# Next-row maxima on a transformer kernel: one 128-row product each, or pairs of 48-row products

## The reference

```python
xn = layernorm(x)
# branch 1: causal attention with a bump instead of a softmax, 16 heads of 8
pressure = q @ k.T * scale ; pressure = where(causal, -10000, pressure)
energy = (pressure - phase_threshold) / (softplus(compressibility) + 1e-6)
attn = 1 - tanh(energy) ** 2 ; attn /= attn.sum(-1) + 1e-6
s = (attn @ v) @ Wo.T
# branch 2: softmax attention (16 heads of 8), then a mixture of experts
h = rmsnorm(xn, norm1_w)
X = xn + softmax(q2 @ k2.T * scale) @ v2 @ wo
h2 = rmsnorm(X, norm2_w)
# shared expert, plus the top 2 of 8 experts weighted by a softmax of their probabilities
ffn = X + swiglu_shared(h2) + sum_e combine[:, e] * swiglu_e(h2)
out = x + s * silu(ffn)
```

## Time and profile before

| | us |
|---|---|
| median of 3 runs | 1097.45 (1096.49 to 1097.86) |
| the profiled execution, its own time | 1097.14 |
| its span, first to last instruction | 1095.4 |
| TensorE busy | 990.9 (90%) |
| VectorE busy | 831.4 (76%) |
| ScalarE busy | 646.8 (59%) |
| GpSimd busy | 351.2 (32%) |

### The profile page before, as it was taken

The page is one execution under the profiler, slowest core; times in us unless marked ns, Lnnn a source line. Parts: engine busy times, 40 slices in busy tenths (PEclk is TensorE's granted clock), DMA queues, the critical chain, the costliest instruction groups (busy, mean ns, idle before and its releaser), DMA issues.

```text
span 1095.4 us, 18252 instructions
## 1 busy us (share of the span) xinstructions
PE 990.9 (90%) x6763; PEld 467.3 (43%) x6784; DVE 831.4 (76%) x1684; ACT 646.8 (59%) x882; POOL 351.2 (32%) x211
## 2 busy tenths in 40 slices
PE   4489999899998999889998999989999899988997
PEld 1123464245542455324652346523554245532464
DVE  6885977869776888759878598795977779773962
ACT  3569724786258842698336972379624785258731
POOL 4702443033520355105530154203352033610032
PEclk9589999999999999999999999999999999999999
DMA  7350561023700435105331055211471033600020
GB/s 231 71 109 22 111 169 34 21 55 80 190 20 12 99 93 132 30 2 130 112 83 30 2 130 143 51 31 30 101 181 24 21 79 83 163 20 2 1 79 10
DMA packets 60392, 81.83 MB, mean 75 GB/s; under 512 B 8560, under 2 KB 47728, under 8 KB 57296
## 3 DMA queue, kind: packets, MB, share of 16 engines
q1 hardware_dynamic: 56544, 75.61, 28.3%
q10 hardware_dynamic: 3760, 5.05, 1.4%
HBM read 52.98 MB, written 27.39 MB: 73 GB/s over the span
## 4 chain that ended last, share of the span: by engine, by line
PE 53%; DVE 25%; ACT 12%; issue 4%; DMA 2%; SPq 1%; ACTq 0%; POOL 0%; DVEq 0%; POOLq 0%
PE O L1156 11%; DVE nmax L758 10%; DVE PT L813 9%; PE O L1139 7%; ACT PT L613 7%; PE S L1172 6%; PE S L1174 5%; PE S L1173 5%; PE S L1112 4%; PE M L1075 3%; PE M L1054 2%; PE M L1080 1%; PE O L1075 1%; SPq L368 1%; DMA stackQ<-mTZ 1%
## 5 line engine op out<-in xcount | busy, mean ns | idle before, releaser
L613 ACT ACTIVATE PT<-S 128x1024 f32<-128x1024 f32 (+1 forms) x448 | 417.0, 967 | 113.7 <-PE S L1112 108.7
L813 DVE SCALAR_TENSOR_TENSOR PT<-PT 128x768 f32<-128x768 f32 (+1 forms) x192 | 213.4, 1163 | 101.0 <-ACT PT L613 101.0
L758 DVE TENSOR_REDUCE nmax<-M 128x1 f32<-128x512 f32 x329 | 218.2, 684 | 43.2 <-PE M L1075 28.3
L1139 PE MATMUL O<-PT,V 128*32 128x256 f32 (+3 forms) x2816 | 246.5, 430 | 0.0
L494 POOL TENSOR_TENSOR PT<-PT,CB 128x1024 f32<-128x1024 f32 x56 | 133.6, 2392 | 261.2 <-DVE PT L951 146.9
L646 ACT ACTIVATE PT<-S 128x1024 f32<-128x1024 f32 x72 | 73.9, 1027 | 241.4 <-PE S L1174 241.4
L479 POOL TENSOR_TENSOR split<-split,parts 128x512 f32<-128x512 f32 x30 | 90.9, 3029 | 372.0 <-ACT parts L573 372.0
L1112 PE MATMUL S<-stackQ,stackK 64*128 64x512 bf16 (+3 forms) x1024 | 166.3, 347 | 9.5 <-DMA stackQ<-mTZ 5.3
L758 DVE TENSOR_REDUCE nmax<-O 128x1 f32<-128x512 f32 x183 | 125.1, 684 | 36.5 <-PE O L1075 17.6
L1172 PE MATMUL S<-h2hi,wgu_hi 128*128 128x512 f32 x288 | 148.7, 516 | 4.3 <-DVE PT L951 4.2
L1156 PE MATMUL O<-PT,wdn 128*128 128x512 f32 x288 | 142.9, 595 | 0.9
(11 more groups left out here) (198 smaller groups left out, 1044.5 us busy)
## 6 DMA issues: line engine op xcount, KB each, us to landing
CB<-scrC SPq DMA_DIRECT2D x64, 256.0 KB, 5.6
stackQ<-scrQ SPq DMA_DIRECT2D x30, 384.0 KB, 5.5
stackK<-scrK SPq DMA_DIRECT2D x30, 384.0 KB, 6.3
scrQ<-parts SPq DMA_DIRECT2D x32, 192.0 KB, 3.3
scrK<-parts SPq DMA_DIRECT2D x30, 192.0 KB, 5.9
scrQ<-parts SPq DMA_DIRECT2D x32, 128.0 KB, 3.4
scrK<-parts SPq DMA_DIRECT2D x30, 128.0 KB, 5.2
KX<-scrK SPq DMA_DIRECT2D x14, 192.0 KB, 3.4
```

What stands on the lines that cost most here:

```text
L613: a.activation(PT[:, n % SLOTS, 2 * q * w:2 * q * w + 2 * w].rearrange("p (r n) -> p r n", r=2), S[k][:, :].rearrange("p (r n) -> p r n", ...
L758: v.tensor_reduce(nmax[:, h % 2, h // 2, t:t + 1], M[k][:, :], AX.X, ALU.max, negate=True).then_inc(m_read[k], 1)
L813: v.scalar_tensor_tensor(p, p, 1.0, p, ALU.subtract, ALU.mult).then_inc(weighed, 1)
L1139: last = t_.matmul(O[k][32 * q:32 * q + VW, i0:i1], V[:, j, 4 * g + q, :], PT[:, n % SLOTS, w * q + at:w * q + at + i1 - i0], start=(j == ...
```

## The change

The maxima X and W of the next row take the paired form as well, so that `maximum` has one form only. `KX`, its clearing on GpSimd, its semaphore and its two DMAs a row are dropped, and the first maximum of run X waits for `stack["K2"]` in its place. So that no pair is torn over two experts or by another piece of work, run X is spread as 4, 4, 4, 4 over experts 2 to 5 (5, 4, 4, 3 before), and `ctxT1` moves behind the fourth maximum of expert 4.

```diff
-PADDED = 4
-spread(MAX["X"], {EXPERT + e: n for e, n in enumerate((0, 0, 5, 4, 4, 3))})
+spread(MAX["X"], {EXPERT + e: n for e, n in enumerate((0, 0, 4, 4, 4, 4))})
 spread(MAX["W"], {EXPERT + 5 + e: n for e, n in enumerate((2, 6, 6, 2))})
 PLACES[EXPERT + 4].insert(2, "V1")
-PLACES[EXPERT + 4].insert(4, "ctxT1")
+PLACES[EXPERT + 4].insert(5, "ctxT1")
...
-        KX = sb("KX", [128, 2, PADDED, L], bf16)
...
             engine.wait_ge(stored[name], (bt + 1) * STORED)
-            if name == "K2" and (not isinstance(bt, int) or bt > 0):
-                for r in range(2):
-                    engine.dma_start(KX[HALF * r:HALF * r + ROW_ADD, r, :, :],
-                                     scratch[name][r].rearrange("c (d h) n -> (c d) h n", h=HP)[:, 0:PADDED, :]).then_inc(stacked_KX, 16)
             load_heads(engine, name, 0, HP, stacked[name])
...
-            g.memset(KX[:, :, :, :].bitcast(dt.uint32), 0).then_inc(kset, 1)
...
             def maximum(u, it, name):
 
                 _m, h, t = name
-                a, hp = HALF * (h % 2), h // 2
+                hp = h // 2
                 rows_later = name in MAX["X"] or name in MAX["W"]
-                alone = rows_later and u is not FIRST
-                if not alone and h % 2:
+                if h % 2:
                     return
-                banks = [begin(u, ("max", i, t)) for i in ((h,) if alone else (h, h + 1))]
+                banks = [begin(u, ("max", i, t)) for i in (h, h + 1)]
                 if 2 in banks:
                     pe.wait_ge(o_read[1], (it + rows_later) * O_USES[1] + 1)
-                if alone:
-                    t_.matmul(M[banks[0]][:, :], stack["Q2"][:, hp, t * 128:t * 128 + 128], KX[:, h % 2, hp, :],
-                              start=True, stop=True).then_inc(m_full[banks[0]], 1)
-                    return
                 for r, k in enumerate(banks):
                     rows = slice(HALF * r, HALF * r + ROW_ADD)
                     t_.matmul(M[k][:, :], stack["Q2"][rows, hp, t * 128:t * 128 + 128], stack["K2"][rows, hp, :],
                               start=True, stop=True).then_inc(m_full[k], 1)
...
-                            pe.wait_ge(stacked_KX, bt * 32)
+                            pe.wait_ge(stacked["K2"], (bt + 1) * 32)
```

More of the change, by code:

```diff
@@ L272, in program @@
         stacked = {n: sem("stacked" + n) for n in stack}
-        stacked_KX = sem("stacked_KX")
         opened = sem("opened")
@@ L400, in prepare @@
                     sp.wait_ge(setup, 2)
-                    sp.wait_ge(kset, 4)
+                    sp.wait_ge(kset, 3)
                     for name in ("Q1", "K1"):
@@ L517, in row @@
                     weigh_expert(it, e)
-            pool.wait_ge(kset, 4)
+            pool.wait_ge(kset, 3)
             pool.wait_ge(gu_hi, 2)
```

## The result

The changed kernel takes 1110.61 us (median of 4 runs, 1109.14 to 1110.72) against 1097.65 (4 runs, 1096.49 to 1099.26): ratio 1.0114, 95% interval 1.0096 to 1.0131. It is slower by 13.0 us, clear of noise, and inside the stated range of 1101.5 to 1113.5. The forecast was 1107.5, with 0.60 on 1104.5 to 1110.5; the measured median lies 0.1 us above that inner band.

What follows compares the result with a forecast made beforehand. TensorE was taken to bound experts 2 to 8. Pairs +0.80 and waits +0.68 gave +1.5 us a row, times seven +10.4, on 1097.14: 1107.5 us; range 1101.5 to 1113.5, with 0.60 on 1104.5 to 1110.5.

Steps and rivals of the forecast that it cites:

- The bound: Experts 2 to 8: TensorE is busy 43.38 of 44 us, so a shift of the experts' end carries one to one.
- The price of a single and of a pair: In the experts: single 0.23 us, pair 0.51 against 0.46 for two singles; 16 pairs give +0.80 us a row.
- The drain: Around each pair: switching array shape drains the engine; 0.29 us of the pair's 0.51 is the two switches.
- The waits: Experts 2 to 8: pairs needing two of three banks at once raise TensorE's waits from 0.7 to 1.36, +0.68 a row.
- Up f0 of expert 2: TensorE's wait before this product falls to 0.24 us from 0.50, since the pair ahead lies in the old wait.
- maxT_X: TensorE's wait before this product rises to 0.34 us from 0.2, its bank being read only after VectorE's 1.39 us cast.
- The wait in expert 3: Heads 0 and 1, tile 3: the pair waits 0.27 us for a VectorE read that stands behind the `oT1` work.
- my walk: Experts 2 to 8, stepped through with TensorE's step times and VectorE's queue; with pairs it ends at +1.49 us a row.
- What costs nothing: Waiting for `stack["K2"]` (12 us of cover), dropping `KX`'s DMAs and clearing, and moving `ctxT1` by 0.9 us: nothing.
- The switches are not hidden: Denies the rival of hidden switches in the experts: pair 0.23, -4.6 us in all, 1092.5; turning point 0.31; faster: 0.06.
- only the price of the pair counts: Rival, in the experts: all added waits vanish, +0.8 us a row, 1102.7; chance 0.14 for 1101.5 to 1104.5.
- the waits bite harder: Rival, experts 4 to 7: VectorE's order reacts, +2.1 us a row, 1111.8, at twice that 1116; chance 0.14 above 1110.5.

Runs made afterwards that it cites:

- e1: The kernel before, with VectorE's maxima of the next row (runs X and W) reading only 64 of 512 columns: 1096.86 us, ratio 1.0004.
- e2: The changed kernel with the same short reads, 64 of 512 columns in runs X and W of the next row: 1103.92 us, ratio 1.0055 to before.
- e4: The kernel before in its own order, each single of runs X and W of the next row as a lone 48-row product: 1155.06 us, ratio 1.0528.
- e3: The changed kernel's order, banks and waits, each pair as two 128-row products against the zero-padded copy of K: 1105.28 us, ratio 1.0072 to before.
- e5: The changed kernel with the padded copy of K still cleared and loaded but read by nobody: 1108.35 us, ratio 1.0087 to before.
- e6: The changed kernel with only the clearing of the padded copy on GpSimd kept, no transfers: 1112.02 us, ratio 1.0119 to before.
- e9: The changed kernel run once more, unchanged, for a second profile of its start: 1109.46 us (one run).
- e10: The kernel before run once more, unchanged, on the same chip: 1099.17 us (one run).

## Why the prediction was right, and where it was off

**The bound.** Right. TensorE fills experts 2 to 8, and the stretch from the ruler's end to the next row's first gate product is 74.4 us before and 74.5 after (means of seven): what the experts gain in length goes one to one into the row.

**The price of a single and of a pair.** Right, the sign of the result hangs on it. 0.23 and 0.51 were read from edges elsewhere in the trace, and one pair in place reads 0.52. The sum over a row was low: taking the change of waits (0.35) off 1.53 leaves 1.18 for the pairs, where the working had 0.80; the same from e1 and e2, +0.87 with waits of 0.53 in e1 and 0.25 in e2, gives 1.15. Some of it is that a pair is 0.52 rather than 0.51 (0.2 a row), some that a single behind L1156 costs 0.22 (before, a single at 412.46 and the second product behind it, L1173, at 412.91, less one step of 0.23), not 0.23. That split is worked out and not tested by itself, and a part stays open; what the rulers give is the sum: a pair is 0.07 dearer than two singles, where the working had 0.05.

**The drain.** The rule of the Trainium skill ("TensorEngine Tiling (Array Packing)", Key Properties), that a change of tiling mode drains the engine, agrees with e4: 0.26 to 0.27 us for a switch there and back around a lone product. How much of that is emptying the engine and how much a weight load that is no longer hidden, no run separates. The "Up to 2×" of the Trainium skill ("TensorEngine Tiling (Array Packing)", Theoretical Speedup) is borne out within the pair, whose halves start within 0.01 us; with the switches around it the pair is slower than two singles here.

**The waits.** The mechanism was right, the size too high: +0.68 forecast, +0.35 read in one row. Up f0 of expert 2 fell to 0.25 (forecast 0.24), expert 4 has 0.19 (0.25), experts 6 and 7 0.14 and 0.13 (0.13 each), maxT_X 0.17 (0.34). The base of maxT_X was misread: the 1.6 us of the earlier trace rows are not 0.2 in each of eight rows but one wait, in the first row, whose product of L1086 is recorded at 42.34 us with 1.64 of idle time before it. In the later rows TensorE didn't wait there before the change. The wait in expert 3 (0.27) didn't come: TensorE reached that pair later than in my walk, and only e3, where it is earlier, shows it. L759 of run X is 0.77 us where I said it would stay at 1.39: it began later (433.36) against GpSimd's multiplication, and both casts end with that one, at 434.13 against 431.72 + 2.37 = 434.09 here and at 428.25 against 428.22 before. The Trainium skill ("TensorEngine Tiling (Array Packing)", Gotcha 1: PSUM Pressure) says that row tiling raises the pressure on PSUM; the trace agrees, with 0.66 us a row that vanish when the reads are short (e1, e2). In e3 two 128-row products that claim two banks at once, without row tiling, cost 0.86.

The two errors, 0.38 too little for the pairs and 0.33 too much for the waits, cancel: +1.49 forecast and +1.53 measured a row, 10.4 and 10.7 us in all. That the sum came so close is luck; the sign and the two mechanisms are not.

**What costs nothing.** Right by e5 and e6 for the transfers and the clearing. The move of `ctxT1` was not run by itself.

**The 13.0 instead of 10.7.** The medians are 2.3 us further apart than seven rulers. 0.5 is between the rulers in the profile after; the rest I can't assign. The start moves an execution by 2 us or more, in either kernel (e9, e10), and with 4 runs each the interval (10.5 to 14.4 us) reaches down to 10.7.

**The rivals.** The switches are not hidden: the pair is at 0.52, far from the 0.31 at which the sign would turn. That only the price of the pair counts is refuted by e2 and e3: the banks cost as well. That the waits bite harder didn't happen: in the row shown L943 ends a wait of TensorE only before up f0 of expert 2. The median of 1110.61 lies in that rival's band of times all the same, by 0.1 us, for the start's sake or by noise and not by its mechanism.

## What to carry to other kernels

Two half-height products that run side by side save one stream, 0.23 us here for 512 columns, and a stay in the other array shape costs 0.27 to 0.29: the pair pays only where the shape is changed anyway, or, by the same numbers and not run here, where several pairs share one stay. Look for both edges of such a stay in the trace before the change, and read them from starts and from the first record that is longer than its kind. And for work that needs two banks at once out of three, look at what the reader does in between and not only at the number of banks: with the switch taken away, order and banks still cost 0.86 us a row.

## What the runs showed of the hardware that was not expected

The time from the first instruction to the first row's experts differs by 1.9 and 2.7 us between two executions of one program (129.1 and 131.0 us for the kernel before, 128.5 and 131.2 for the changed one), along with the length of the stretch at 1.2 GHz: it ended at 67.9 us in the profile after and is over by 62 in e9.

A lone product of 48 rows costs twice a product of 128 rows between 128-row neighbours (0.50 against 0.23 us), although it reads less. And two costs that are 0.87 and 0.86 when alone add up to only 1.53 us a row: for 0.20 of it the switches delay TensorE where it would otherwise have waited for VectorE.
